# Cross-attention on one core: the last tile's second half stored as two pieces of 64 lines, from two queues

## The reference, cut to what matters

```python
Q = (img_embed @ Wq).reshape(B, -1, H, D).transpose(0, 2, 1, 3)      # B 2, 2048 queries, H 8, D 512
K = (sent_embed @ Wk).reshape(B, -1, H, D).transpose(0, 2, 1, 3)     # 77 keys
V = (sent_embed @ Wv).reshape(B, -1, H, D).transpose(0, 2, 1, 3)
score = jnp.einsum('bhqd,bhkd->bhqk', Q, K) / math.sqrt(D)
attn = jax.nn.softmax(jnp.where(mask, score, -jnp.inf), axis=-1)
ctx = jnp.einsum('bhqk,bhkd->bqhd', attn, V).reshape(B, -1, H * D)
out = ctx @ Wo + img_embed
mu = jnp.mean(out, axis=-1, keepdims=True)
var = jnp.var(out, axis=-1, keepdims=True)
return (out - mu) * jax.lax.rsqrt(var + EPS) * gamma + beta          # (2, 2048, 512) float32
```

## Time and profile before

| what | us |
|---|---|
| three runs | 355.99, 355.93, 355.36 |
| median | 355.93 |
| the profiled execution, its own time | 354.91 |
| its span, first to last instruction | 353.1 |
| PE busy | 347.5 |
| DVE busy | 265.1 |
| ACT busy | 228.6 |
| POOL busy | 193.0 |

### The profile page before, as it was taken

One profiled execution on the slowest core, in us unless ns is written; L12 is line 12 of the kernel. 1 busy time (PEld: TensorE's weight loads), 2 busy tenths in 40 slices (PEclk: granted clock), 3 DMA queues, 4 the chain that ended last, 5 costly groups with the idle time before them and its releaser, 6 DMA issues. The chain is left out here.

```text
span 353.1 us, 6783 instructions
## 1 busy us (share of the span) xinstructions
PE 347.5 (98%) x2272; PEld 323.9 (92%) x2272; DVE 265.1 (75%) x495; ACT 228.6 (65%) x778; POOL 193.0 (55%) x208
## 2 busy tenths in 40 slices
PE   9999999999999999999999999999999999999994
PEld 6999999999999999998899899988988998899884
DVE  2159998673921277898798988987988989879896
ACT  3267764244333569887876976878768769778560
POOL 0045640000003857679679688687696796885243
PEclk9999999999999999999999999999999999999999
DMA  8999779775735070052242341541522413403003
GB/s 236 425 420 337 255 240 338 274 250 211 228 137 202 0 278 22 3 179 97 84 151 70 137 152 38 172 137 43 180 90 91 149 65 144 148 32 120 32 35 114
DMA packets 19682, 55.80 MB, mean 158 GB/s; under 512 B 1728, under 2 KB 3264, under 8 KB 17728
## 3 DMA queue, kind: packets, MB, share of 16 engines
q1 hardware_dynamic: 18784, 54.38, 42.8%
q10 hardware_dynamic: 864, 1.00, 1.1%
HBM read 46.98 MB, written 8.39 MB: 157 GB/s over the span
## 5 line engine op out<-in xcount | busy, mean ns | idle before, releaser
L646 PE MATMUL pair<-vw_hi,pt_hi 128*128 128x512 f32 x155 | 62.2, 402 | 0.0
L646 PE MATMUL pair<-vw_hi,pt_lo 128*128 128x512 f32 x155 | 60.9, 393 | 0.0
L646 PE MATMUL pair<-vw_lo,pt_hi 128*128 128x512 f32 x155 | 60.5, 391 | 0.0
L1250 POOL TENSOR_TENSOR out_sb<-centred,beta_sb 128x512 f32<-128x512 f32 x30 | 38.8, 1294 | 28.9 <-ACT centred L840 28.8
L1270 POOL TENSOR_TENSOR x_sum<-xt_in 128x256 f32<-128x256 f32 x16 | 11.9, 745 | 62.2 <-DMA xt_in<-x_tiles 62.1
L795 ACT ACTIVATE prob<-c,neg_max 128x77 f32<-128x77 f32 x128 | 44.0, 346 | 0.0
L1295 POOL TENSOR_TENSOR xo_lo<-x_sum,xo_hi 128x512 fp32r<-128x512 f32 x32 | 41.6, 1304 | 0.5 <-ACT xo_hi L819 0.5
L571 PE MATMUL pair<-a_hi,xo_hi 128*128 128x308 f32 x128 | 40.4, 316 | 0.0
L571 PE MATMUL pair<-a_hi,xo_lo 128*128 128x308 f32 x128 | 38.9, 304 | 0.0
L571 PE MATMUL pair<-a_lo,xo_hi 128*128 128x308 f32 x128 | 38.9, 304 | 0.0
L833 ACT ACTIVATE pt_hi<-pair 128x640 fp32r<-128x640 f32 x32 | 22.5, 703 | 23.5 <-PE pair L633 23.5
(11 more groups left out here) (119 smaller groups left out, 945.0 us busy)
## 6 DMA issues: line engine op xcount, KB each, us to landing
w_out<-wo SPq DMA_DIRECT2D x8, 1024.0 KB, 4.8
xt_in<-x_tiles SPq DMA_DIRECT2D x16, 512.0 KB, 3.8
x_in<-x_rows SPq DMA_DIRECT2D x16, 512.0 KB, 4.8
out<-out_sb SPq DMA_DIRECT2D x31, 256.0 KB, 2.2
w_out<-wq_t SPq DMA_DIRECT2D x7, 1024.0 KB, 7.8
w_proj<-wv SPq DMA_DIRECT2D x8, 768.0 KB, 4.7
w_proj<-wk SPq DMA_DIRECT2D x6, 768.0 KB, 9.6
w_out<-wq_t SPq DMA_DIRECT2D x2, 512.0 KB, 7.9
```

What stands on the lines that cost most here:

```text
L646: mm = pe.matmul(ps_out[:, i % 2, 0:s.model], ps[:, j, :], v[:, b, j, :], start=(j == 0 and n == 0), stop=(j == s.key_t - 1 and n == len(p ...
L1250: pool.tensor_tensor(out_sb[i % OUT_RING][:, :], centred[i % 2][:, :], beta_sb[:, :], ALU.add)\
```

## The change

The second half of the last tile is no longer one DMA from ACT. ACT stores lines 0 to 63 of it, and SP, after its store of the first half and a wait for `dve_last` 3, stores lines 64 to 127. Both count on `stored_last`, and the final wait asks for both.

```diff
@@ -443,6 +443,9 @@
                     sp.wait_ge(dve_last, 2)
                     sp.dma_start(out[t * P:(t + 1) * P, 0:COLS], out_sb[t % OUT_RING][:, 0:COLS])\
                       .then_inc(stored[t % OUT_RING], DMA_INC)
+                    sp.wait_ge(dve_last, 3)
+                    sp.dma_start(out[t * P + P // 2:T * P, COLS:s.model],
+                                 out_sb[t % OUT_RING][P // 2:P, COLS:s.model]).then_inc(stored_last, DMA_INC)
                 elif t >= 0:
                     sp.wait_ge(pool_out, t + 1)
                     if t == LAST - 1:
@@ -451,7 +454,7 @@
                       .then_inc(stored[t % OUT_RING], DMA_INC)
             for n in range(OUT_RING):
                 sp.wait_ge(stored[n], DMA_INC * len(range(n, T, OUT_RING)))
-            sp.wait_ge(stored_last, DMA_INC)
+            sp.wait_ge(stored_last, 2 * DMA_INC)
@@ -913,8 +916,8 @@
             scale(T - 3)
             scale_first_half(T - 2)
             act.wait_ge(dve_last, 3)
-            act.dma_start(out[LAST * P:T * P, COLS:s.model], out_sb[LAST % OUT_RING][:, COLS:s.model])\
-               .then_inc(stored_last, DMA_INC)
+            act.dma_start(out[LAST * P:LAST * P + P // 2, COLS:s.model],
+                          out_sb[LAST % OUT_RING][0:P // 2, COLS:s.model]).then_inc(stored_last, DMA_INC)
```

## The result

| | kernel before | changed kernel |
|---|---|---|
| median of 22 runs each, us | 355.71 | 356.12 |
| profiled execution, own time, us | 354.91 | 356.61 |
| its span, us | 353.1 | 354.8 |
| last `finish` ends, us | 350.85 | 351.95 |
| from there to the span's end (the *tail*), us | 2.25 | 2.85 |

The ratio is 1.0017, 95% interval 1.001 to 1.0023: slower by 0.6 us, between 0.36 and 0.82 (the two medians alone lie 0.41 apart). The change is resolved from zero. The forecast had been 355.9, no change.

The account below looks back on a forecast made before the run. PE bounds the kernel, working 347.5 of 353.1 us; the change can touch only 1.7 us after its last matmul. Terms 0 + 0 - 0.04 + 0.02 + 0 = -0.02 us on 355.93 gave 355.9 us, range 355.5 to 356.5.

Parts of the forecast that it names:

- What bounds the kernel, and where the change can act: After PE's last matmul: only the 1.7 us between the last store's issue and its landing can move.
- ACT's DMA of 64 lines, cost 0: ACT's last store: issue stays at 350.88; a possible 0.17 us shorter issue gains nothing, as ACT has nothing behind it.
- SP's new wait, cost 0: SP after its first-half store: waits 0.04 us, issues at about 350.88 beside ACT, ends at 351.21; cost 0.
- Packets, -0.04: Second half's 128 KB on the same 16 engines: only the idle share between stores can be won, -0.04 us.
- 0.85 + 0.5 + 0.35 us: Last store: issue to first packet, packets, last packet to landing; only the 0.5 us depends on lines moved.
- Completion packets, +0.02: Last store in two pieces: 32 small packets instead of 16, one more on each engine, +0.02 us.
- Starting stores together, 0 between +0.45 and -0.23: Three stores started within 0.4 us at the end: up to 0.45 us later or 0.23 sooner, taken as 0.
- Rival A: Last store: landing time goes with DMA size and pieces run side by side; end moves -0.15 us, to 355.8; chance 0.12.
- Rival B: Last stores: queues issuing at once are served in turn; +0.2 to +0.45 us, 356.1 to 356.4; chance 0.13.
- Rival C: SP's second store is held until its first lands; +1.1 to +1.3 us, 357.0 to 357.2; chance 0.02.
- its own sign: Wrong if SP's last wait, measured from the last `finish`'s end, changes over 0.5 us, or anything ahead of that `finish` moves.
- The bound of 0.2%: Whole kernel: a measurement can tell about 0.2%, 0.7 us, from no change; chance 0.91 of landing within it.

Follow-up runs that it names:

- cut at 48: Against the changed kernel: second half cut at line 48, ACT storing 48 lines and SP 80; ratio to the kernel before 1.0006, tail 2.50 us.
- cut at 96: Against the changed kernel: second half cut at line 96, ACT storing 96 lines and SP 32; ratios to the kernel before 0.9999 and 1.0005.

## Why the prediction was wrong

The tails make a ladder. It orders the kernels; no step but the last is a change of one thing:

| kernel | tail, us | step |
|---|---|---|
| before, two profiles | 2.25, 2.30 | |
| two pieces of 128 lines by columns | 2.33 | a second piece and queue, packets of 512 bytes: 0.05 |
| cut at 48, cut at 96 | 2.50, 2.60 | by lines instead of by columns: 0.2 |
| changed, two profiles | 2.85, 2.84 | the cut moved to 64 and 64: 0.3 |

The sum, 0.57 us, is what the timed runs say, 0.6. Of the single steps, the timed runs confirm only that the first two together are small: by columns 1.0005, cut at 48 1.0006, cut at 96 0.9999 and 1.0005, changed 1.0017 and 1.0018.

- *What bounds the kernel, and where the change can act*: right. Nothing ahead of the last `finish` depends on it, and the closing work kept its length, 0.5 us.
- *ACT's DMA of 64 lines, cost 0*: **this is the step that failed.** Its place in the code was right, issue 0.03 us after DVE; its price was not. I bounded it from below, by a saving of 0.17 us, and from above by nothing, though the trace before held no DMA of 64 lines at all. It cost 0.2 us more to issue and 0.3 us more to start. Alone on ACT, with half the bytes, it lengthened the tail by 0.25 us. The price of 64 lines was shown on ACT alone, on SP alone, and in 18 stores amid the kernel.
- *SP's new wait, cost 0*: right for the wait and the issue's instant. The issue itself, priced at 0.33 from a store on an idle queue, took 0.72 and 0.61, and its first packet came after 1.5 us instead of 0.85: the same failed step, and the piece that ends last.
- *Packets, -0.04*: wrong. I held that engines 0.98 busy at 332 GB/s would move the same 128 KB at the same rate. With two pieces they moved them at 187 GB/s, at 0.79 busy, behind a hole of 0.3 us. In part that is because SP's piece joins 0.3 us after ACT's; in part each packet is slower, 0.070 us instead of 0.048. That 0.85 + 0.5 + 0.35 us had only one part that depends on the number of lines was a reading of stores that all had 128.
- *Completion packets, +0.02*: the working is wrong. One of the four packets of the slice was a 1 KB one of 0.048 us, and I shared its time among all four. The slice from 353.9 above has four small ones alone: 2.1% of 16 x 0.1 us, 0.008 us each. Whether the term is +0.01 or nothing is not resolved.
- *Starting stores together, 0 between +0.45 and -0.23*: 0.17 us for two DMAs of 128 lines, 0.3 for SP's piece beside ACT's of 64. These fall inside the bound; the value taken did not. The slices of the earlier trace rows allow 0.4 to 0.6 us, so the 0.45 was not their outer end.
- *Rival A* (smaller lands sooner): falls. 64 KB landed in 2.0 us alone, 128 KB in 1.7. The Trainium skill's fit in the size, page "DMA: Bandwidth & Descriptors", section "Anatomy of one DMA — SWDGE (gpsimd) path", is for DMAs that GpSimd issues, and these come from SP and ACT; the gain of 0.15 us estimated from it has the wrong sign for these stores. The rule of the Trainium skill, page "DMA: Bandwidth & Descriptors", section "Rules for kernel authors", not to bother with two disjoint halves, held, and the price was more than the nothing that I read into it.
- *Rival B* (the two queues served in turn): part of it is seen, a first packet later than 1 us and a hole in the share, but the hole lies ahead of both pieces and not between them. The most that it allowed was +0.45, the runs showed +0.6. *Rival C* falls: SP's last wait was 1.5 us, not 2.9. With the whole second half on SP, the second store's packets began at 352.7, while the first, issued at 351.27, landed only 1.7 us later, at 353.0.
- By its own sign the prediction was wrong: measured from the end of the last `finish`, SP's last wait ended after 1.75 us before and after 2.35 in the changed kernel, 0.6 us more where 0.5 was the limit.
- The predicted 355.9 is only 0.2 us below the 356.12 measured, and that is luck: it was added to the 355.93 of three runs, and the median of 22 runs of the same kernel is 355.71. The forecast difference was -0.02, the measured one +0.6. The time lies inside the range, but the range reached up by the +0.45 of starting together and by scatter; it held nothing for a DMA of 64 lines. Rival B's 356.1 meets the number with another mechanism. The bound of 0.2% put the change, at 0.17%, among the cases without one.

Shown: that the count of 64 costs at the issue and the start, at three first lines, two widths, on both queues; that stores of one half of the lines, or of lines from 0 on, move fewer bytes a second at the same share. Not shown: why 64, why those lines are slower, and how much of SP's issue of 0.61 to 0.72 us is the count, as 80 lines took 0.69 in the same place. Loads of 64 lines were not tried.

No version beat the kernel before. The nearest are the two pieces by columns, 1.0005 with a tail of 2.33, and the cut at line 96, 0.9999 and 1.0005 with a tail 0.3 us longer than before.

## What to carry to other kernels

When a change gives a DMA a new shape, its price can't be read from DMAs of another shape, even at half the size: bound it upward too, or measure it in one kernel that stores in several counts. Keep a last store at all 128 lines, split it by columns if it must be split (no split gained anything here), and read each issue's own duration as well as the gaps. A kernel's tail, from the last computed value to the end, resolves 0.05 us where single runs of one kernel lie up to 1.3 apart (355.01 to 356.29).

## What the runs showed of the hardware that was not expected

- A store of exactly 64 lines took 0.47 to 0.49 us to issue on SP amid the kernel (0.55 to 0.57 across the middle and for the first one of each run, 0.54 on ACT) and 1.12 to 1.23 us to its first packet. 16, 32, 48, 80, 96, 112 and 128 lines took 0.31 to 0.37 us, and their first packet came after 0.81 to 0.87.
- A store of 128 lines moved 369 GB/s with 2 KB packets; stores of lines 0 to 31, 0 to 63 and 0 to 95 moved 215, 205 and 246 and one of lines 64 to 127 moved 232, all with the 16 engines over 0.9 busy. A store of lines 32 to 95, also 64 lines, moved 348.
- At the kernel's end, a store 0.4 us behind another of SP's queue took 0.54 to 0.58 us to issue instead of 0.33, with 128 lines too, and 0.69 with 80 lines beside an issue of ACT's. A load 0.47 us behind a store amid the kernel took 0.39 instead of 0.37.
- Two queues that issued 128 lines each at one instant lost 0.17 us on one of them.
